# First similarities and maxima of the last stage laid into the end of the middle stage, and its first two silus of the dense layer moved behind ScalarE's first change of table

## The chip, the cores and the metric

The kernel runs on one core of one Trainium2 chip. The metric is the device time of one execution in microseconds (us). A core has five engines that run their own instruction streams and meet at semaphores: TensorE (PE in the rows, with PEld for its weight loads), VectorE (DVE), ScalarE (ACT), GpSimd (POOL) and SyncE (SP), which here only issues transfers. Each engine takes its instructions strictly in the order of its stream.

## The reference

Four residual blocks over 32 sequences of 128 tokens with 128 features. The first two are a cross-attention over a context of 77 and a layer of 16 routed experts. The change lies where the third block ends and the fourth begins:

```python
x = x + _L1_xattn_ref(_layernorm(x), ctx_1024, ctx_1024)        # the middle stage
x = x + _L1_ffn_ref(_layernorm(x), W_up, W_down, W_q, keys, down_embed, up_embed)   # the last stage

# _L1_xattn_ref
scores = jnp.einsum('bqd,bkd->bqk', query, key) * d ** (-0.5)
...
attn = jax.nn.softmax(scores, axis=-1)
return jnp.einsum('bqk,bkd->bqd', attn, value)

# _L1_ffn_ref: 4 heads, two sets of 64 keys, 8 best of each, 8 best of the 64 sums
q = jnp.einsum('btd,ed->bte', hidden_states, W_q)
...
sim = jnp.einsum('pbthn,hkpn->pbthk', q, keys)
scores_xy, idx_xy = jax.lax.top_k(sim, K)
...
scores, pk = jax.lax.top_k(all_scores, K)
indices = jnp.take_along_axis(all_idx, pk, axis=-1)
de = down_embed[indices]
ue = up_embed[indices]
w = jax.nn.silu(jnp.einsum('btd,bthkd->bthk', hidden_states, de) * jax.nn.softmax(scores, axis=-1))
experts_states = jnp.einsum('bthk,bthkd->btd', w, ue)
dense = jnp.einsum('bti,di->btd', jax.nn.silu(jnp.einsum('btd,id->bti', hidden_states, W_up)), W_down)
return dense + experts_states
```

## The kernel before

All orders are written out by hand, one stream for each engine; every buffer is kept twice and `p` (0 or 1) names the copy.

**The middle stage** walks over 8 groups `g` of 4 sequences. TensorE transposes the tokens (`tokens_t`), makes the scores against the context (`scores(g)`), transposes the exponentials (`probabilities_t`) and applies them (`attention`). ScalarE makes the exponentials (`exps(g)`), takes the transposes out of PSUM and computes the reciprocal roots of the next normalisation (`roots3(g)`). VectorE adds the result to the tokens (`add_attention`) and takes their statistics (`statistics3`). GpSimd normalises the tokens of groups 0 to 6 (`last_tokens(g)`, L501); VectorE does that of group 7 (`last_tokens(7)`, L1543). TensorE transposes them (`last_tokens_t(g)`, L1119) and ScalarE writes them to `x3_t` (`last_tokens_out(g)`), which raises `xt3_ready`.

**The last stage** handles 32 tiles of 128 tokens, two in a turn, in 16 turns. For tile `(i, p)`, in the order in which the data flows:

- SyncE copies the tile's columns from `x3_t` into `xt[p]` (`load_d`); for turn `i` it waits until `score_mm` says that the scores of turn `i - 1` have been made from the old `xt[p]`.
- TensorE: `keys` (L1146, all similarities in one matmul), `scores` (L1161) and `last_scores` (L1167), `up` (L1154, the dense layer's first matmuls), `down` (L1179), `back` (L1189, transposes of the weights), `add_experts` (L1198).
- ScalarE: `similarities` (L762 and L552, a part of `keys`' result to SBUF), `exps(i, p)` (L783), `silus` (L791, four heads), `hidden` (L769, the silu of `up`'s result into `h1[p]`). Exponential and silu need different tables, so each turn holds two ACT_TABLE_LOADs (L807, L813).
- VectorE: `near_tops` (L1573 to L1581, the eight best of each head), `best_pairs` (L1598 to L1606), `own_sums` (L1588), `pick` (L1616), `norms`, `tail` (L1629), `result` (L1635).
- GpSimd: `sums` (L512) and `weigh` (L520).

Three dependences matter here. `up(i + 1, p)` writes the bank from which `hidden(i, p)` reads, so it waits for `h1_ready`. `hidden(i + 1, p)` overwrites `h1[p]`, so it waits for `down_mm`, that is, for `down(i, p)`. And ScalarE's turn runs `similarities(i + 1, 1)`, then `exps(i, 1)`, then the change to silu:

```python
            if more:
                similarities(i + 1, 1)
            exps(i, 1)
            act.preload_act_table(ACT.Silu)
            silus(i, 0)
            if more:
                hidden(i + 1, 0)
                hidden(i + 1, 1)
                silus(i, 1)
```

Ahead of turn 0 stand the first `similarities`, the first two `hidden` and a first `exps(0, 0)`; as the roots of the middle stage use the table with logarithm and exponential, the two `hidden` are framed by two loads of their own (L769, L824).

Of the kernel before, what the change touches and what calls it, by code (L numbers as in the profile page):

```python
# [87 lines left out]
def program(nc, a):  # L88
    with ExitStack() as ctx:
# [448 lines left out]
        def _(act):  # L538
# [199 lines left out]

            tokens_out(0)
            roots2(0)  # L740
            tokens_out(1)
            roots2(1)
            for g in range(NB):
                exps(g)
                if g >= 3:
                    last_tokens_out(g - 3)
                if g + 2 < NB:
                    tokens_out(g + 2)
                if g + 2 < NB:
                    roots2(g + 2)  # L750
                probabilities_out(g)
                if g:
                    roots3(g - 1)
            last_tokens_out(NB - 3)
            last_tokens_out(NB - 2)
# [85 lines left out]
        def _(pe):  # L841
# [279 lines left out]

            tokens_t(0)
            tokens_t(1)
            scores(0)
            scores(1)
            tokens_t(2)
            for g in range(NB):
                probabilities_t(g)
                if g + 2 < NB:
                    scores(g + 2)  # L1130
                attention(g)
                if g >= 2:
                    last_tokens_t(g - 2)
                if g + 3 < NB:
                    tokens_t(g + 3)
            last_tokens_t(NB - 2)


            pe.wait_ge(wts_d, 64)

# [115 lines left out]
        def _(dve):  # L1256
# [291 lines left out]
            statistics2(0)
            statistics2(1)
            maximum(0)  # L1550
            biases(0)
            maximum(1)
            biases(1)
            statistics2(2)
            for g in range(NB):
                if g:
                    add_attention(g - 1)
                    statistics3(g - 1)
                shares(g)
                if g + 3 < NB:  # L1560
                    statistics2(g + 3)
                if g + 2 < NB:
                    maximum(g + 2)
                    biases(g + 2)
            add_attention(NB - 1)
            statistics3(NB - 1)
            last_tokens(NB - 1)
# [133 lines left out]
```

## Time and profile before

| | |
|---|---|
| time, median of 3 runs | 469.45 us (469.17 to 470.87) |
| time of the profiled execution | 469.85 us |
| its span from first to last instruction | 468.1 us |
| busy: PE, DVE, ACT, POOL | 401.9, 359.4, 332.9, 336.2 us |
| mean granted TensorE clock | 0.96 of full speed |

The span is what the trace shows; 1.75 us of the profiled execution's time lie outside it. The middle stage ends and the last stage begins between 200 and 240 us. Busy shares over the whole span say little about that stretch; it is read from the instructions in order of time.

### The profile page before, as it was taken

The numbers are of one execution on the slowest core, as the hardware profiler recorded it, in microseconds if no ns is written. First come the engines' busy times: TensorE is split into PE (matmuls) and PEld (weight loads), VectorE is DVE, ScalarE is ACT, GpSimd is POOL, SyncE is SP. The second block draws the span as 40 slices with busy tenths as digits, with TensorE's granted clock in tenths as the row PEclk, the third lists the DMA queues.
The fourth block names the chain that finished last, engine by engine and source line by source line (L and its number), as shares of the span: only waits on it lengthen the run. The fifth ranks groups of instructions, "written<-read, shape, count | busy, mean of one in ns | idle before, by whom it ended". The sixth has DMA issues, their size and how long they took to land.

```text
span 468.1 us, 9533 instructions
## 1 busy us (share of the span) xinstructions
PE 401.9 (86%) x2617; PEld 322.8 (69%) x2617; DVE 359.4 (77%) x1473; ACT 332.9 (71%) x606; POOL 336.2 (72%) x266
## 2 busy tenths in 40 slices
PE   4899898599999787867889988998899988999876
PEld 3687786278998656754666777777767777767766
DVE  3799887323233269976999999999999999999981
ACT  2466353244445057656699999999999999999994
POOL 5226666614655605571899999999999999999993
PEclk9999999599999999869799999999999999999998
DMA  6998022126876160000000000000000000000000
GB/s 186 336 274 242 30 75 92 47 50 201 218 201 190 45 181 7 6 1 12 1 13 23 22 11 15 19 22 22 11 11 22 22 17 16 12 22 22 13 11 13
DMA packets 46515, 32.02 MB, mean 68 GB/s; under 512 B 4155, under 2 KB 42651, under 8 KB 46491
## 3 DMA queue, kind: packets, MB, share of 16 engines
q1 hardware_dynamic: 42635, 25.01, 18.8%
q0 software_dynamic: 2624, 6.43, 3.9%
q10 hardware_dynamic: 1232, 0.31, 0.3%
q8 instruction: 10, 0.16, 0.2%
q14 instruction: 14, 0.11, 0.1%
HBM read 19.02 MB, written 10.62 MB: 63 GB/s over the span
## 4 chain that ended last, share of the span: by engine, by line
POOL 33%; issue 10%; DVE 7%; PE 4%; ACT 3%; POOLq 1%; ACTq 0%; DVEq 0%
POOL arena_sb L520 21%; POOL arena_sb L512 11%; DVE picked_sb L1616 4%; ACT arena_sb L791 1%; PE banks L1146 1%; PE banks L1189 1%; PE banks L1154 1%; POOL xh_sb L501 1%; PE banks L1179 0%; ACT arena_sb L783 0%; PE banks L1198 0%; PE banks L1248 0%; DVE arena_sb L1588 0%; ACT sc_sb L724 0%; POOLq L524 0%
## 5 line engine op out<-in xcount | busy, mean ns | idle before, releaser
L520 POOL TENSOR_TENSOR arena_sb<-arena_sb,picked_sb 128x1096 f32<-128x1096 f32 (+1 forms) x46 | 151.8, 3331 | 10.1 <-DVE picked_sb L1616 10.1
L1616 DVE SCALAR_TENSOR_TENSOR picked_sb<-arena_sb,best_sb,banks 128x548 f32<-128x548 f32 x128 | 90.3, 777 | 0.2 <-POOL arena_sb L512 0.2
L791 ACT ACTIVATE arena_sb<-arena_sb,bsum_sb 128x548 f32<-128x548 f32 x124 | 83.0, 743 | 8.3 <-DVE bsum_sb L1624 7.3
L512 POOL TENSOR_TENSOR arena_sb<-near_sb,sim_y_sb 128x1024 f32<-128x1024 f32 (+1 forms) x32 | 74.1, 2340 | 10.2 <-DVE near_sb L1581 10.2
L1189 PEld LDWEIGHTS banks<-ident_sb,arena_sb 128*128 128x128 f32 x496 | 57.9, 153 | 24.5 <-issue 16.2
L1189 PE MATMUL banks<-ident_sb,arena_sb 128*128 128x128 f32 x496 | 61.9, 279 | 4.8 <-DVE arena_sb L1629 4.8
L783 ACT ACTIVATE arena_sb<-arena_sb 128x2192 f32<-128x2192 f32 x32 | 65.6, 2049 | 0.2
L490 POOL DMA_INDIRECT token_rows<-arena_sb,token_of_sb x32 | 30.7, 960 | 33.4 <-issue 24.7
L1154 PEld LDWEIGHTS banks<-xt_sb,w_up_t_sb 128*128 128x128 f32 x256 | 32.8, 200 | 19.5 <-ACT w_t_sb L552 17.6
L1179 PE MATMUL banks<-w_down_t_sb,h_sb 128*128 128x128 f32 x256 | 36.0, 286 | 8.9 <-DVE x_all_sb L1635 8.9
L1154 PE MATMUL banks<-xt_sb,w_up_t_sb 128*128 128x128 f32 x256 | 36.9, 290 | 6.7 <-ACT w_t_sb L552 6.0
L449 POOL DMA_INDIRECT slot_rows<-x_all_sb,scatter_row_sb x32 | 31.4, 983 | 13.7 <-issue 9.5
L1198 PE MATMUL banks<-up_e_sb,w_t_sb 128*128 128x128 f32 x256 | 35.3, 281 | 5.5 <-DVE picked_sb L1616 4.5
L501 POOL TENSOR_SCALAR xh_sb<-x_all_sb,cmv_sb,crstd_sb 128x128 f32<-128x128 f32 x28 | 21.9, 792 | 25.1 <-ACT crstd_sb L714 25.1
L1458 DVE TENSOR_SCALAR arena_sb<-banks 128x512 f32<-128x512 f32 x16 | 11.1, 691 | 36.7 <-PE banks L1036 36.7
L1179 PEld LDWEIGHTS banks<-w_down_t_sb,h_sb 128*128 128x128 f32 x256 | 31.5, 194 | 11.1 <-issue 11.1
L1146 PE MATMUL banks<-z_sb,xt_sb 128*128 128x512 f32 x64 | 34.7, 628 | 3.1 <-DVE arena_sb L1588 2.3
L1198 PEld LDWEIGHTS banks<-up_e_sb,w_t_sb 128*128 128x128 f32 x256 | 31.0, 191 | 8.5 <-DVE picked_sb L1616 5.2
L1161 PE MATMUL banks<-down_t_sb,xt_sb 128*128 128x512 f32 x64 | 31.3, 612 | 0.0
L1036 PE MATMUL banks<-arena_sb,w_sb 128*128 128x256 f32 x128 | 29.9, 382 | 1.0 <-ACT arena_sb L552 1.0
L1046 PE MATMUL banks<-w_sb,arena_sb 128*128 128x128 f32 x256 | 30.5, 275 | 0.0
L1588 DVE TENSOR_TENSOR arena_sb<-near_sb,banks 128x1024 f32<-128x1024 f32 (+1 forms) x32 | 30.1, 939 | 0.0
(188 smaller groups left out, 826.5 us busy)
## 6 DMA issues: line engine op xcount, KB each, us to landing
w_sb<-w SPq DMA_DIRECT2D x32, 256.0 KB, 3.4
slot_rows<-arena_sb POOLq DMA_DIRECT2D x4, 528.0 KB, 6.4
arena_sb<-slot_rows SPq DMA_DIRECT2D x16, 132.0 KB, 2.3
x_all_sb<-x SPq DMA_DIRECT2D x8, 256.0 KB, 3.7
token_rows<-x_all_sb SPq DMA_DIRECT2D x8, 256.0 KB, 2.8
x_all_sb<-token_rows SPq DMA_DIRECT2D x8, 256.0 KB, 5.1
xt_sb<-x_t_sb SPq DMA_DIRECT2D x32, 64.0 KB, 1.8
out<-x_all_sb SPq DMA_DIRECT2D x32, 64.0 KB, 1.5
```

Source lines behind the costliest of these rows:

```text
L449: pool.indirect_dma_start(out=slots, out_offset=bass.IndirectOffsetOnAxis(ap=scatter_row[i % 2][:, t:t + 1], axis=0), in_=x_all[:, i * TT ...
L512: pool.tensor_tensor(vv[p][:, 0:n, 0:DENSE].rearrange("p h (i j) -> p h i j", i=XI), near[p][:, 0:n, TOP:2 * TOP].unsqueeze(3).broadcast_t ...
L520: pool.tensor_tensor(pp[p][:, heads, :], pp[p][:, heads, :], picked[p][:, heads, :], ALU.mult).then_inc(weighed, 1)
L783: act.activation(pp[p][:, :, :], vv[p][:, :, 0:WIDE], ACT.Exp).then_inc(pp_ready, 1)
L791: ins = act.activation(pp[p][:, h, :], pp[p][:, h, :], ACT.Silu, scale=bsum[p][:, h:h + 1])
L1146: pe.matmul(bank[4 * p + 1][:, :], xt[p][:, :], z1[:, :], start=True, stop=True).then_inc(sim_mm, 1)
L1154: ins = pe.matmul(bank[4 * p][:, c * P:(c + 1) * P], w_up_t[:, c * P:(c + 1) * P], xt[p][:, :], start=True, stop=True)
L1161: ins = pe.matmul(bank[4 * p + 2][:, :], xt[p][:, :], down_t[:, :], start=True, stop=True)
L1179: ins = pe.matmul(results(p), h1[p][:, c, :], w_down_t[:, c, :], start=c == 0, stop=False)
L1189: ins = pe.matmul(bank[4 * p][0:n, c * P:(c + 1) * P], pp[p][:, h, c * P:c * P + n], ident[:, :], is_transpose=True, start=h == 0, stop=h ...
L1198: ins = pe.matmul(results(p), w_t[p][:, c, :], up_e[:, c, :], start=False, stop=c == FC - 1)
L1616: ins = dve.scalar_tensor_tensor(out=picked[p][:, h, :], in0=vv[p][:, h, 0:WIDE], scalar=best[p][:, h, TOP - 1:TOP], in1=scores_of(p), op0 ...
```

## The change

It moves instructions and adds no arithmetic. VectorE, ScalarE and TensorE get a new order between the last groups of the middle stage and the second turn of the last one; the loops of the later turns stay as they are. The functions keep their bodies, apart from the names `context_scores` for the middle stage's `scores` and `exps_of_tables` for the last stage's `exps`. GpSimd's and SyncE's streams are untouched. The core of the diff (definitions that only moved are left out):

```diff
 # ScalarE
             def turn(i, j, more, most=True):
...
                 act.preload_act_table(ACT.Silu)
+                if i is FIRST:
+                    hidden(FIRST, 0)
+                    hidden(FIRST, 1)
                 silus(i, 0)
...
+            similarities(FIRST, 0)
             last_tokens_out(NB - 3)
+            similarities(FIRST, 1)
             last_tokens_out(NB - 2)
...
-            similarities(FIRST, 0)
-            similarities(FIRST, 1)
             roots3(NB - 1)
             last_tokens_out(NB - 1)
-            hidden(FIRST, 0)
-            hidden(FIRST, 1)
-            act.preload_act_table(ACT.Exp)
-            exps(FIRST, 0)
+            exps_of_tables(FIRST, 0)
             similarities(1, 0)
             turn(0, None, True)
 # TensorE
+            for g in range(NB):
+                probabilities_t(g)
+                if g + 2 < NB:
+                    context_scores(g + 2)
+                attention(g)
+                if g >= 2:
+                    last_tokens_t(g - 2)
+                if g + 3 < NB:
+                    tokens_t(g + 3)
+                if g >= NB - 2:
+                    pe.wait_ge(cexp_ready, g + 1)
+                    keys(FIRST, g - (NB - 2))
+            last_tokens_t(NB - 2)
+            pe.wait_ge(wts_d, 64)
             for p in two:
                 scores(FIRST, p)
             last_tokens_t(NB - 1)
+            pe.wait_ge(xt3_ready, NB - 1)
+            up(FIRST, 0)
+            last_scores(0, first=True)
+            keys(1, 0)
             pe.wait_ge(xt3_ready, NB)
-            for p in two:
-                up(FIRST, p)
-                last_scores(p, first=True)
-            keys(1, 0)
+            up(FIRST, 1)
+            last_scores(1, first=True)
             keys(1, 1)
             turn(FIRST, None, True)
 # VectorE
+            near_tops(FIRST, 0)
             add_attention(NB - 1)
             statistics3(NB - 1)
+            best_pairs(FIRST, 0)
+            own_sums(FIRST, 0)
             last_tokens(NB - 1)
...
-            step.turn()
-            for p in two:
-                near_tops(FIRST, p)
-                best_pairs(FIRST, p)
-                own_sums(FIRST, p)
+            near_tops(FIRST, 1)
+            best_pairs(FIRST, 1)
+            own_sums(FIRST, 1)
             pick(FIRST, 0)
             pick(FIRST, 1)
```

**ScalarE, from `last_tokens_out(7)` into turn 0.** Line numbers are those of either file; `h_sb` is `hidden`, the first `arena_sb` row with 128x2192 is the exponential of tile (0, 0), `first_sb` and `sim_y_sb` are `similarities`, `bsum_sb` marks `silus`. Before:

```order
L552 ACTIVATE x_t_sb<-banks 128x512
L769 ACT_TABLE_LOAD
L769 ACTIVATE h_sb<-banks 128x512 x2
L824 ACT_TABLE_LOAD
L783 ACTIVATE arena_sb<-arena_sb 128x2192
L762 ACTIVATE first_sb<-banks 128x4x8
L552 ACTIVATE sim_y_sb<-banks 128x128
L775 ACTIVATE bexp_sb<-best_sb 128x32 x2
L762 ACTIVATE first_sb<-banks 128x4x8
L552 ACTIVATE sim_y_sb<-banks 128x192
L783 ACTIVATE arena_sb<-arena_sb 128x2192
L807 ACT_TABLE_LOAD
```

and from the same place in the changed kernel:

```order
L552 ACTIVATE x_t_sb<-banks 128x512
L764 ACTIVATE arena_sb<-arena_sb 128x2192
L743 ACTIVATE first_sb<-banks 128x4x8
L552 ACTIVATE sim_y_sb<-banks 128x128
L756 ACTIVATE bexp_sb<-best_sb 128x32 x2
L743 ACTIVATE first_sb<-banks 128x4x8
L552 ACTIVATE sim_y_sb<-banks 128x192
L764 ACTIVATE arena_sb<-arena_sb 128x2192
L788 ACT_TABLE_LOAD
L750 ACTIVATE h_sb<-banks 128x512 x2
L772 ACTIVATE arena_sb<-arena_sb,bsum_sb 128x548 x4
```

Two table loads are gone, and the first two `hidden` now stand behind `exps(0, 1)` and the load of turn 0, ahead of `silus(0, 0)`.

**TensorE, from the first `up` to the first `down`.** `w_up_t_sb` is `up`, 128x36 is `last_scores`, `z_sb` is `keys`, `w_down_t_sb` is `down`. Before:

```order
L1154 MATMUL banks<-xt_sb,w_up_t_sb 128x128 x4
L1167 MATMUL banks<-down_t_sb,xt_sb 128x36
L1154 MATMUL banks<-xt_sb,w_up_t_sb 128x128 x4
L1167 MATMUL banks<-down_t_sb,xt_sb 128x36
L1146 MATMUL banks<-z_sb,xt_sb 128x512 x2
L1154 MATMUL banks<-xt_sb,w_up_t_sb 128x128 x8
L1179 MATMUL banks<-w_down_t_sb,h_sb 128x128 x4
```

and in the changed kernel:

```order
L1134 MATMUL banks<-xt_sb,w_up_t_sb 128x128 x4
L1147 MATMUL banks<-down_t_sb,xt_sb 128x36
L1126 MATMUL banks<-z_sb,xt_sb 128x512
L1134 MATMUL banks<-xt_sb,w_up_t_sb 128x128 x4
L1147 MATMUL banks<-down_t_sb,xt_sb 128x36
L1126 MATMUL banks<-z_sb,xt_sb 128x512
L1134 MATMUL banks<-xt_sb,w_up_t_sb 128x128 x8
L1159 MATMUL banks<-w_down_t_sb,h_sb 128x128 x4
```

`keys(1, 0)` now stands between the two halves of `up` and `last_scores`, so `last_scores` of tile (0, 1), whose end lets SyncE load `xt[1]` for `keys(1, 1)`, is queued behind a matmul that itself waits for a load.

**VectorE, from `add_attention(7)` on.** `csum_sb` marks `add_attention`, the next two rows are `statistics3`, `xh_sb` is `last_tokens(7)`, `first_sb` begins `near_tops`. Before:

```order
L1533 SCALAR_TENSOR_TENSOR x_all_sb<-banks,csum_sb,x_all_sb 128x128 x4
L1487 BN_STATS cbn_sb<-x_all_sb 128x6 x4
L1490 BN_AGGR cmv_sb<-cbn_sb 128x2 x4
L1543 TENSOR_SCALAR xh_sb<-x_all_sb,cmv_sb,crstd_sb 128x128 x4
L73 ISA
L1573 MAX first_sb<-banks 128x8 x4
L1576 MAX banks<-banks 128x8 x4
```

and in the changed kernel, where `near_tops(0, 0)` has already ended in the row ahead:

```order
L1531 SCALAR_TENSOR_TENSOR x_all_sb<-banks,csum_sb,x_all_sb 128x128 x4
L1485 BN_STATS cbn_sb<-x_all_sb 128x6 x4
L1488 BN_AGGR cmv_sb<-cbn_sb 128x2 x4
L1573 TENSOR_TENSOR arena_sb<-near_sb,banks 128x4x2x8
L1576 TENSOR_TENSOR arena_sb<-near_sb,banks 128x4x28 x2
L1581 MAX best_sb<-arena_sb 128x8 x4
L1563 TENSOR_TENSOR arena_sb<-near_sb,banks 128x2x512
L1541 TENSOR_SCALAR xh_sb<-x_all_sb,cmv_sb,crstd_sb 128x128 x4
L1548 MAX first_sb<-banks 128x8 x4
```

The work of tile (0, 0) has moved ahead of `last_tokens(7)`, in two pieces around `add_attention(7)` and `statistics3(7)`.

## Rows read from the trace of the kernel before

**Rows 1.** The page's chain that ended last, share of the span by engine.
```profile
POOL 33%; issue 10%; DVE 7%; PE 4%; ACT 3%; POOLq 1%; ACTq 0%; DVEq 0%
```

**Rows 2.** Timeline of VectorE, later turns: start, length (us), line, tiles, [idle before <-releaser].
```profile
237.76 0.31 DVE L1629 TENSOR_REDUCE arena_sb<-arena_sb 128x1 f32<-128x148 f32 x1
238.26 5.65 DVE L1616 SCALAR_TENSOR_TENSOR picked_sb<-arena_sb,best_sb,banks 128x548 f32<-128x548 f32 x8 [0.18 <-POOL arena_sb L512]
...
253.21 5.65 DVE L1616 SCALAR_TENSOR_TENSOR picked_sb<-arena_sb,best_sb,banks 128x548 f32<-128x548 f32 x8
```

**Rows 3.** Timeline of GpSimd.
```profile
206.82 3.12 POOL L501 TENSOR_SCALAR xh_sb<-x_all_sb,cmv_sb,crstd_sb 128x128 f32<-128x128 f32 x4 [0.52 <-ACT crstd_sb L714]
...
256.16 9.80 POOL L520 TENSOR_TENSOR arena_sb<-arena_sb,picked_sb 128x2192 f32<-128x2192 f32 x3 [0.54 <-DVE picked_sb L1616]
```

**Rows 4.** Timeline of VectorE between the stages.
```profile
208.41 1.12 DVE L1533 SCALAR_TENSOR_TENSOR x_all_sb<-banks,csum_sb,x_all_sb 128x128 f32<-128x128 f32 x4 [1.69 <-PE banks L1107]
...
214.65 1.11 DVE L1543 TENSOR_SCALAR xh_sb<-x_all_sb,cmv_sb,crstd_sb 128x128 f32<-128x128 f32 x4 [3.70 <-ACT crstd_sb L714]
215.68 0.58 DVE L1573 MAX8 first_sb<-banks 128x8 f32<-128x56 f32 x4
...
217.75 0.22 DVE L1598 TENSOR_TENSOR arena_sb<-near_sb,banks 128x64 f32<-128x64 f32 x1
...
218.78 1.20 DVE L1588 TENSOR_TENSOR arena_sb<-near_sb,banks 128x1024 f32<-128x1024 f32 x1
219.90 0.58 DVE L1573 MAX8 first_sb<-banks 128x8 f32<-128x56 f32 x4
...
223.57 5.65 DVE L1616 SCALAR_TENSOR_TENSOR picked_sb<-arena_sb,best_sb,banks 128x548 f32<-128x548 f32 x8
```

**Rows 5.** Timeline of ScalarE between the stages.
```profile
217.13 1.28 ACT L769 ACT_TABLE_LOAD   x1
218.43 0.60 ACT L769 ACTIVATE h_sb<-banks 128x512 f32<-128x512 f32 x1
...
220.10 1.28 ACT L824 ACT_TABLE_LOAD   x1
...
225.88 0.20 ACT L762 ACTIVATE first_sb<-banks 128x32 f32<-128x32 f32 x1 [1.97 <-PE banks L1146]
...
226.19 2.03 ACT L783 ACTIVATE arena_sb<-arena_sb 128x2192 f32<-128x2192 f32 x1
...
231.52 2.68 ACT L791 ACTIVATE arena_sb<-arena_sb,bsum_sb 128x548 f32<-128x548 f32 x4 [2.00 <-DVE bsum_sb L1624]
...
235.06 2.68 ACT L791 ACTIVATE arena_sb<-arena_sb,bsum_sb 128x548 f32<-128x548 f32 x4
```

**Rows 6.** Timeline of TensorE between the stages; each matmul counts as two instructions.
```profile
204.41 1.13 PE L1098 MATMUL banks<-ident_sb,sc_sb 128*77 128x128 f32 x4
...
209.99 1.11 PE L1119 MATMUL banks<-ident_sb,xh_sb 128*128 128x128 f32 x4 [0.83 <-POOL xh_sb L501]
...
217.17 1.16 PE L1154 MATMUL banks<-xt_sb,w_up_t_sb 128*128 128x128 f32 x8 [0.69 <-ACT x_t_sb L552]
218.16 0.31 PE L1167 MATMUL banks<-down_t_sb,xt_sb 128*128 128x36 f32 x2
...
220.39 1.13 PE L1146 MATMUL banks<-z_sb,xt_sb 128*128 128x512 f32 x2 [0.80 <-DMA xt_sb<-x_t_sb]
223.80 2.05 PE L1146 MATMUL banks<-z_sb,xt_sb 128*128 128x512 f32 x2 [2.28 <-DVE arena_sb L1588]
225.64 3.62 PE L1154 MATMUL banks<-xt_sb,w_up_t_sb 128*128 128x128 f32 x16
```

**Rows 7.** Windows: stretch, length, busy us and count of PE, PEld, DVE, ACT, POOL, clock.
```profile
212.00:213.00 1.00, 1.00 (x2) 0.39 (x2) 0.00 (x0) 0.16 (x2) 0.00 (x0) 0.58 0.00 0
...
222.00:224.00 2.00, 0.20 (x1) 0.23 (x2) 1.97 (x9) 1.91 (x5) 2.00 (x1) 0.77 0.00 0
...
228.00:230.00 2.00, 2.00 (x11) 2.00 (x11) 1.97 (x8) 1.50 (x2) 2.00 (x1) 0.53 0.00 0
```

More of the change, by code:

```diff
@@ L737, in last_tokens_out @@
                      bank[4 * (g % 2)][:, :].rearrange("p (b t) -> p b t", b=BT))
[L739 to L755, printed above, removed]
             def similarities(i, p):
@@ L775, in best_exps, with exps_of_tables @@
                     act.activation(bexp[p][:, :, :], best[p][:, :, :], ACT.Exp).then_inc(bexp_ready, 1)
-            def exps(i, p):
+            def exps_of_tables(i, p):
                 act.wait_ge(best_ready, 1 + 2 * i + p + 1)
@@ L805, in turn @@
                     similarities(i + 1, 1)
-                exps(i, 1)
+                exps_of_tables(i, 1)
                 act.preload_act_table(ACT.Silu)
+                if i is FIRST:
+                    hidden(FIRST, 0)
+                    hidden(FIRST, 1)
                 silus(i, 0)
@@ L813, in turn @@
                     act.preload_act_table(ACT.Exp)
-                    exps(i + 1, 0)
+                    exps_of_tables(i + 1, 0)
                     if most:
                         similarities(i + 2, 0)
+            tokens_out(0)
+            roots2(0)
+            tokens_out(1)
+            roots2(1)
+            for g in range(NB):
+                exps(g)
+                if g >= 3:
+                    last_tokens_out(g - 3)
+                if g + 2 < NB:
+                    tokens_out(g + 2)
+                if g + 2 < NB:
+                    roots2(g + 2)
+                probabilities_out(g)
+                if g:
+                    roots3(g - 1)
             similarities(FIRST, 0)
+            last_tokens_out(NB - 3)
             similarities(FIRST, 1)
+            last_tokens_out(NB - 2)
             roots3(NB - 1)
             last_tokens_out(NB - 1)
-            hidden(FIRST, 0)
-            hidden(FIRST, 1)
-            act.preload_act_table(ACT.Exp)
-            exps(FIRST, 0)
+            exps_of_tables(FIRST, 0)
             similarities(1, 0)
@@ L1079, in tokens_t, with context_scores @@
                 ins.then_inc(cxnt_mm, 1)
-            def scores(g):
+            def context_scores(g):
                 p = g % 2
@@ L1120, in last_tokens_t @@
                 ins.then_inc(xt3_mm, 1)
[L1122 to L1139, printed above, removed]
             def keys(i, p):
@@ L1222, in turn @@
                         keys(i + 2, 1)
-            pe.wait_ge(cexp_ready, NB)
-            keys(FIRST, 0)
-            keys(FIRST, 1)
+            tokens_t(0)
+            tokens_t(1)
+            context_scores(0)
+            context_scores(1)
+            tokens_t(2)
+            for g in range(NB):
+                probabilities_t(g)
+                if g + 2 < NB:
+                    context_scores(g + 2)
[9 more added lines that the diff above has]
+            pe.wait_ge(wts_d, 64)
             for p in two:
@@ L1545, in last_tokens @@
                 ins.then_inc(cxh_ready, 1)
-            step.turn()
[L1548 to L1567, printed above, removed]
             def near_tops(i, p):
@@ L1659, in _ @@
             step.turn()
-            for p in two:
-                near_tops(FIRST, p)
-                best_pairs(FIRST, p)
-                own_sums(FIRST, p)
+            statistics2(0)
+            statistics2(1)
+            maximum(0)
+            biases(0)
+            maximum(1)
+            biases(1)
+            statistics2(2)
+            for g in range(NB):
+                if g:
+                    add_attention(g - 1)
+                    statistics3(g - 1)
+                shares(g)
+                if g + 3 < NB:
+                    statistics2(g + 3)
+                if g + 2 < NB:
+                    maximum(g + 2)
+                    biases(g + 2)
+            near_tops(FIRST, 0)
+            add_attention(NB - 1)
+            statistics3(NB - 1)
+            best_pairs(FIRST, 0)
+            own_sums(FIRST, 0)
+            last_tokens(NB - 1)
+            near_tops(FIRST, 1)
+            best_pairs(FIRST, 1)
+            own_sums(FIRST, 1)
             pick(FIRST, 0)
```

## The prediction, made from these rows

> **What bounds the kernel now.** I began with the chain that ended last: GpSimd has the largest share of it [rows 1]. That is only the last link seen from the end, so I looked at one whole turn. `pick`, the last piece of VectorE's turn, starts at 238.26 and again at 253.21 us [rows 2]: a turn lasts 14.95 us. GpSimd's `weigh` waits 0.54 us in it for `pick` [rows 3], while VectorE, at its worst place in the first turn, waits 0.18 us [rows 2]. So VectorE sets the pace, by a small margin. The change leaves the loops alone; every later turn starts 14.95 us after the one before, and the end moves by as much as `pick(1, 0)` at 238.26 moves. The question is when that instruction can start.
>
> Then I read the timelines of the four engines between 204 and 240 us. VectorE stands idle 3.70 us ahead of `last_tokens(7)` and 1.69 us ahead of `add_attention(7)` [rows 4]: there is room for the work that the change moves. ScalarE makes two table loads of 1.28 us, but later waits 1.97 us for `keys(1, 1)` and 2.00 us for the norms [rows 5]. TensorE waits for a transfer ahead of `keys(1, 0)` and for VectorE's `own_sums(0, 1)` ahead of `keys(1, 1)` [rows 6]. Last come the clocks: TensorE is at half its speed (1.2 GHz) until about 212.84, at 2.4 GHz until about 223.08, and low again until about 229.88; the three times follow from means of 0.58, 0.77 and 0.53 in windows that hold one step each [rows 7].
>
> **The change, part by part.**
>
> *VectorE's tile (0, 0) moved up.* `keys(0, 0)` goes ahead of `probabilities_t(7)`, which starts at 204.41. At the lower clock `keys` takes the stream 1.84 us (223.80 to 225.64), at the higher one about half [rows 6]. I take 1.7. What stands behind it is late by that: `roots3(6)`, and GpSimd's `last_tokens(6)` goes from 206.82 to about 208.5 [rows 3]. `similarities(0, 0)` take 0.3 (225.88 to 226.19 [rows 5]), so `near_tops(0, 0)` starts near 208.9. Its 2.07 us (215.68 to 217.75 [rows 4]) end at 211.0. `add_attention(7)` then starts at 211.0 in place of 208.41; with the statistics it takes 2.54 (208.41 to 210.95, where the wait of 3.70 begins), to 213.5. `best_pairs` and `own_sums` of tile (0, 0), 2.15 (217.75 to 219.90), end at 215.7, `last_tokens(7)`, 1.03, at 216.7, and tile (0, 1), 3.67 (219.90 to 223.57), at 220.4. `pick(0, 0)` would start 3.2 us early (223.57 before). `last_tokens(7)` itself ends 1.0 late. `keys(0, 1)` pushes back `last_tokens_t(6)` too, but the roots behind it are due at 216, so that is covered; without this cover it would cost up to a `keys`, 1.84. The `sums` of GpSimd and SyncE's stream keep their order and cost nothing: GpSimd idles until `near_tops` is done in either kernel.
>
> *TensorE's `keys(1, 0)` between the two `up`.* After `last_tokens(7)` come four transposes, about 0.6 (1.11 at the lower clock [rows 6]), to 217.3. `up(0, 0)` no longer waits 0.69 for `last_tokens_out(7)`; its 0.99 (217.17 to 218.16) end at 218.3. From there to `keys(1, 0)` 2.23 us pass (218.16 to 220.39: `last_scores`, SyncE's issue and the transfer), to 220.5. `keys` takes about 1.0, `up(0, 1)` 0.99, to 222.5, and now the same 2.23 come a second time, because `last_scores(1)`, which frees `xt[1]`, was queued behind `keys(1, 0)`: `keys(1, 1)` starts at 224.7. It was 223.80. The lead of 3.2 us on VectorE is lost on this chain of two transfers. `keys(1, 1)` ends at 225.8 at the higher clock (1.13) or 226.7 at the lower (2.05); before, 225.85.
>
> *ScalarE.* Two loads go, 2 x 1.28 = 2.56 us of its own time [rows 5]. But `exps(0, 1)` stands behind `similarities(1, 1)`, which wait for `keys(1, 1)`. So it starts at 226.15 or 227.1 (226.19 before), and the saved loads turn into a longer wait there. `exps(0, 1)` and the load end 3.35 later (2.03 and 1.28), then come both `hidden`, 0.60 each and overlapping a little, 1.05 together. `silus(0, 0)` starts at 230.55 or 231.45 (231.52 before) and ends 2.68 later, at 233.2 or 234.1.
>
> The Trainium skill, page "ScalarE: Activation LUTs", section "What ACT_TABLE_LOAD costs", counts a drain of about 1.38 us on top of a load of 1.28, and its rules ask for batching by table. By that the change would save 5.3 us of ScalarE's time. The rows have no such drain: the load at 217.13 ends at 218.41 and the silu starts at 218.43 [rows 5]. By either price it is time in which ScalarE would wait for `keys(1, 1)`.
>
> *The dense layer behind it.* This is the part that I expect to decide. `up(1, 0)` waits for `hidden(0, 0)`, which now ends at 230.1 or 231.0. Before, `up(1, 0)` and `up(1, 1)` ran from 225.64 for 3.62 us [rows 6] and `down` behind them, well ahead of `hidden(1, 0)`. Now `up(1, 0)`, `up(1, 1)` and `down(0, 0)` must pass between `hidden(0, 0)` and `hidden(1, 0)`, and `down(0, 1)` ahead of `hidden(1, 1)`. Each is a group of four matmuls, 0.99 at the higher clock and 1.81 (3.62 / 2) at the lower. TensorE has nothing to do from the end of `keys(1, 1)` until then, over 4 us; before, 1.13 us of matmul between waits of 0.80 and 2.28 were enough for the clock to fall [rows 6, 7]. So these groups start low. How long they stay low is bounded by the two returns in the trace: 2.8 us after gapless work began (209.99 to 212.84) and 6.1 us (223.80 to 229.88) [rows 6, 7].
>
> With `hidden(0, 0)` at 230.1 and the clock back after 2.8 us: 1.55 groups at 1.81, then 1.45 at 0.99, 0.15 for the result to land: `down(0, 0)` is done at 234.5, `last_scores` and `down(0, 1)` 1.15 later, `hidden(1, 1)` 0.55 after that. `silus(0, 1)` starts at 236.2 against 235.06: +1.1. With the clock back after 6.1 us it is 237.55: +2.5. If `keys(1, 1)` was low, both are 0.9 more: +2.0 and +3.4.
>
> From there nothing changes: `silus(0, 1)`, 2.68, then `tail(0, 1)` at 237.76 and `pick(1, 0)` at 238.26 [rows 2], all later by the same amount. `weigh(0, 1)`, for which the second half of these silus waits, starts behind `exps(0, 1)` by 228.2 to 229.2 and takes half of 9.80 [rows 3], to 233.1 to 234.1: no wait.
>
> **Sum.** -3.2 on VectorE, used up by the second transfer; -2.56 on ScalarE, used up by the same wait; +1.1 to +3.4 from `up` and `down` on the path. The middle of the four values is 2.25; I take +2.1, since 1.7 for `keys(0, 0)` is near its upper end. On the profiled execution's 469.85 that makes 471.95. That execution is 0.4 above the median of the runs shown, 469.45; on the median it is **471.5**.
>
> **Rivals.**
>
> *The lower clock comes earlier.* From 213 on TensorE's work is thinner than before: a wait for `last_tokens(7)`, then two transfers. If it falls to 1.2 GHz already there, `up(0, 0)`, `keys(1, 0)` and `up(0, 1)` cost 0.8 to 0.9 more each. For it: the fall at 223.08. Against: `up` and `keys` still fill a good part of that stretch. Two of the three add 1.7, in all +3.8: 473.3. The Trainium skill, page "TensorE: Matmul & The Clock Gate", section "Loop structure matters more than you think", warns of just this, matmuls with a transfer to wait for between them; the trace of before has one such place, and the clock fell behind it.
>
> *The clock is back at once, or doesn't fall.* Then three groups take 3.1 and fit beside `silus(0, 0)`, and `silus(0, 1)` moves by -0.1 to +0.8: about 469.8. Against it: over 4 us without a matmul.
>
> *Faster: the saved loads count.* If `keys(1, 1)` came early enough that ScalarE need not wait for it, `exps(0, 1)` would start up to 2.6 earlier and the whole turn with it: 466.9. It decides from the point where the second transfer takes under about half of its 2.23, and the groups behind `hidden(0, 0)` run at the higher clock. By the skill's drain it would be up to 5.3, 464.2. Against both: the one such transfer in the trace took 2.23.
>
> *Nothing moves.* The later turns could take back a part: GpSimd's wait of 0.54 is such a slack, VectorE's stream shows none. About 469.5.
>
> **How the numbers follow.** The forecast (+1.1 to +3.4) gets 0.60, the lower clock earlier 0.16, the clock back at once 0.14, faster 0.06, nothing 0.04. The bound of 0.5%, about what a measurement of this kernel can tell from no change, is 2.35 us: 467.1 and 471.8. Of the forecast, 0.24 lie above 471.8 and 0.36 below. Slower: 0.24 + 0.16 = 0.40. Same: 0.36 + 0.14 + 0.04 = 0.54. Faster: 0.06. The range leaves out the faster case and the upper half of the earlier clock: 469.0 to 473.5; the forecast's own is 470.5 to 472.9.
>
> **What would show it.** Right: `pick(0, 0)` near 220, `keys(1, 1)` waiting for a transfer of `xt` and starting at 224 or later, ScalarE idle some 3 to 5 us ahead of `similarities(1, 1)`, ScalarE's silus of `hidden(1, *)` waiting for L1159, the clock low around 230, `pick(1, 0)` at 239.4 to 241.7, and turns of 14.95 after it. Wrong: `keys(1, 1)` before 223, a clock of 1.00 at 230 to 234, no wait ahead of `hidden(1, 0)`, or turns of another length, which would mean that the pace is set by what I have not looked at.

## The result, and the profile after

The changed kernel takes 473.05 us in the median of 17 runs (468.70 to 475.06), the kernel before 469.73 beside it (467.71 to 471.85, 17 runs). The ratio of times is 1.0045, with a 95% interval of 1.0023 to 1.0066: about 2.1 us slower. The two medians stand 3.3 us apart; as the runs of either kernel scatter over 4 to 6 us, I go by the ratio and its interval. The forecast was 2.1 us slower, 471.5 in a range of 469.0 to 473.5.

The profiled execution took 474.34 us, 4.5 more than the one of before (469.85), which is twice the ratio. The first thing to settle is therefore how much of it lies in the stretch that was changed. The edit begins behind `probabilities_t(6)`, so I look there first, on TensorE's timeline of the kernel before:

```profile
97.32 3.69 PE L1036 MATMUL banks<-arena_sb,w_sb 128*128 128x256 f32 x16
...
200.62 0.66 PE L1098 MATMUL banks<-ident_sb,sc_sb 128*77 128x128 f32 x4 [1.35 <-ACT sc_sb L724]
```

TensorE's timeline after; the lines of the program have moved up by two here:

```profile
97.46 5.38 PE L1034 MATMUL banks<-arena_sb,w_sb 128*128 128x256 f32 x16
...
202.64 0.66 PE L1096 MATMUL banks<-ident_sb,sc_sb 128*77 128x128 f32 x4 [1.57 <-ACT sc_sb L724]
...
218.61 0.66 PE L1117 MATMUL banks<-ident_sb,xh_sb 128*128 128x128 f32 x4 [1.94 <-DVE xh_sb L1541]
219.10 1.06 PE L1134 MATMUL banks<-xt_sb,w_up_t_sb 128*128 128x128 f32 x8
...
222.21 1.13 PE L1126 MATMUL banks<-z_sb,xt_sb 128*128 128x512 f32 x2 [1.91 <-DMA xt_sb<-x_t_sb]
223.17 1.05 PE L1134 MATMUL banks<-xt_sb,w_up_t_sb 128*128 128x128 f32 x8
...
226.31 1.12 PE L1126 MATMUL banks<-z_sb,xt_sb 128*128 128x512 f32 x2 [1.93 <-DMA xt_sb<-x_t_sb]
231.77 3.78 PE L1134 MATMUL banks<-xt_sb,w_up_t_sb 128*128 128x128 f32 x16 [4.34 <-ACT h_sb L750]
235.34 1.91 PE L1159 MATMUL banks<-w_down_t_sb,h_sb 128*128 128x128 f32 x8
```

`probabilities_t(6)` is 2.02 us late before the edit has had any effect. Most of it arises at 97 us, in the expert layer of the second block: the same 16 instructions take 5.38 us in place of 3.69. TensorE's clock was at half there, as the last section shows. So I count every time of after from `probabilities_t(6)`: 2.02 is taken off before it is compared. From there to `pick(1, 0)` this profile has 39.66 us against 37.64 (238.26 [rows 2] less 200.62): **+2.02**.

The rows above show how. `keys(1, 0)` waits 1.91 us for a transfer, `keys(1, 1)` 1.93 us for the next one, and then TensorE waits 4.34 us for ScalarE's `h_sb`, that is for `hidden(0, 0)`; before, `up` followed `keys(1, 1)` without a gap [rows 6]. What became of the two waits on ScalarE's own timeline after:

```profile
223.37 0.20 ACT L743 ACTIVATE first_sb<-banks 128x32 f32<-128x32 f32 x1 [1.56 <-PE banks L1126]
...
227.47 0.20 ACT L743 ACTIVATE first_sb<-banks 128x32 f32<-128x32 f32 x1 [3.50 <-PE banks L1126]
...
227.78 2.03 ACT L764 ACTIVATE arena_sb<-arena_sb 128x2192 f32<-128x2192 f32 x1
229.82 1.28 ACT L788 ACT_TABLE_LOAD   x1
231.12 1.08 ACT L750 ACTIVATE h_sb<-banks 128x512 f32<-128x512 f32 x2
232.09 2.67 ACT L772 ACTIVATE arena_sb<-arena_sb,bsum_sb 128x548 f32<-128x548 f32 x4
237.35 0.60 ACT L750 ACTIVATE h_sb<-banks 128x512 f32<-128x512 f32 x1 [2.59 <-PE banks L1159]
238.88 0.60 ACT L750 ACTIVATE h_sb<-banks 128x512 f32<-128x512 f32 x1 [0.93 <-PE banks L1159]
239.37 2.67 ACT L772 ACTIVATE arena_sb<-arena_sb,bsum_sb 128x548 f32<-128x548 f32 x4
```

The two table loads of before are gone. ScalarE waits 3.50 us for `keys(1, 1)`, where it waited 1.97 [rows 5], and `exps(0, 1)` is 0.43 us earlier than before (227.78 - 2.02 = 225.76 against 226.19). Then come the new waits, 2.59 and 0.93 us for L1159, `down`. `silus(0, 1)`, the last row, starts 36.73 us after `probabilities_t(6)`; before it was 235.06 - 200.62 = 34.44: +2.29.

VectorE's timeline after:

```profile
210.91 0.59 DVE L1548 MAX8 first_sb<-banks 128x8 f32<-128x56 f32 x4 [1.63 <-ACT sim_y_sb L552]
...
222.15 5.65 DVE L1591 SCALAR_TENSOR_TENSOR picked_sb<-arena_sb,best_sb,banks 128x548 f32<-128x548 f32 x8
...
242.07 0.31 DVE L1604 TENSOR_REDUCE arena_sb<-arena_sb 128x1 f32<-128x148 f32 x1 [4.24 <-ACT arena_sb L772]
242.30 5.64 DVE L1591 SCALAR_TENSOR_TENSOR picked_sb<-arena_sb,best_sb,banks 128x548 f32<-128x548 f32 x8
...
257.65 5.65 DVE L1591 SCALAR_TENSOR_TENSOR picked_sb<-arena_sb,best_sb,banks 128x548 f32<-128x548 f32 x8 [0.32 <-issue]
```

`pick(0, 0)` is 3.44 us earlier (222.15 - 2.02 = 220.13 against 223.57 [rows 4]), and nothing comes of it: the `tail` waits 4.24 us for ScalarE's silus, and `pick(1, 0)` stands behind it. From there to the next `pick` it is 15.35 us, not 14.95; the turns behind it have 14.96, against 14.95 before.

TensorE's clock after, in windows (stretch, length, busy us and count of PE, PEld, DVE, ACT and POOL, clock):

```profile
226.00:228.00 2.00, 1.12 (x2) 0.30 (x2) 2.00 (x6) 0.53 (x3) 2.00 (x1) 0.94 0.00 0
...
230.00:232.00 2.00, 0.23 (x1) 0.23 (x2) 1.90 (x16) 1.99 (x3) 2.00 (x1) 0.50 0.00 0
...
236.00:238.00 2.00, 2.00 (x11) 2.00 (x11) 1.80 (x9) 0.60 (x1) 2.00 (x2) 0.50 0.00 0
238.00:240.00 2.00, 2.00 (x12) 1.42 (x12) 0.00 (x0) 1.12 (x2) 1.53 (x1) 1.00 0.00 0
```

It falls to 1.2 GHz at about 227.8, just behind `keys(1, 1)`, and is back at 238.0, 6.2 us after `up(1, 0)` began. All of `up(1, p)` and most of `down(0, p)` ran at half speed.

### The profile page after: what moved, and what is told of

Read it like the earlier page. It is cut to its first block, busy times and chain, and to the rows that moved or that the text cites. A ratio compares the mean times of both kernels' runs of the same rounds, so it can differ in the third digit from the quotient of the medians.

```text
span 472.6 us, 9530 instructions
## 1 busy us (share of the span) xinstructions
PE 401.9 (85%) x2617; PEld 323.4 (68%) x2617; DVE 359.4 (76%) x1473; ACT 330.2 (70%) x604; POOL 336.3 (71%) x266
## 4 chain that ended last, share of the span: by engine, by line
POOL 32%; issue 10%; DVE 5%; PE 4%; ACT 2%; DMA 1%; POOLq 1%; ACTq 0%
POOL arena_sb L520 21%; POOL arena_sb L512 11%; DVE picked_sb L1591 4%; PE banks L1134 1%; ACT arena_sb L772 1%; ACT arena_sb L764 1%; DMA xt_sb<-x_t_sb 1%; PE banks L1169 1%; PE banks L1159 1%; PE banks L1126 0%; PE banks L1246 0%; PE banks L1178 0%; POOLq L524 0%; PE banks L1141 0%; DVE arena_sb L1563 0%
## 5 line engine op out<-in xcount | busy, mean ns | idle before, releaser
L1159 PE MATMUL banks<-w_down_t_sb,h_sb 128*128 128x128 f32 x256 | 36.8, 290 | 8.9 <-DVE x_all_sb L1610 8.9
L1159 PEld LDWEIGHTS banks<-w_down_t_sb,h_sb 128*128 128x128 f32 x256 | 32.2, 198 | 11.2 <-issue 11.2
L1034 PE MATMUL banks<-arena_sb,w_sb 128*128 128x256 f32 x128 | 31.6, 397 | 1.0 <-ACT arena_sb L552 1.0
```

The costliest lines, as they stand in the source:

```text
L1034: ins = pe.matmul(bank[2 + 2 * (b % 2) + c // 2][:, (c % 2) * CAP:(c % 2 + 1) * CAP], w1[b][:, c * P:(c + 1) * P], xe_t[b % 2][:, :], star ...
L1159: ins = pe.matmul(results(p), h1[p][:, c, :], w_down_t[:, c, :], start=c == 0, stop=False)
```

## The experiments

What I compare is the stretch from `probabilities_t(6)` to `pick(1, 0)` in the profile of each, 37.64 us before and 39.66 after, and the ratio of times to the kernel before, run beside each, with its interval. One profile of each was taken. Two profiles of the changed kernel differ by 1.6 us in the stretch, by TensorE's clock alone, so a stretch is read together with its rows and its ratio, and a difference of a few tenths carries nothing.

**The order on TensorE put back.** The changed kernel, with both `up` ahead of both `keys` again:

```diff
  up(FIRST, 0); last_scores(0, first=True)
- keys(1, 0)
  pe.wait_ge(xt3_ready, NB)
  up(FIRST, 1); last_scores(1, first=True)
+ keys(1, 0)
  keys(1, 1)
```

> The changed kernel with TensorE's old order: both up(0, p) and last_scores(p) first, then keys(1, 0) and keys(1, 1), so that the two transfers of xt overlap. Measured from the start of probabilities_t(6) to that of pick(1, 0): 37.64 us in the kernel before, 39.66 in the changed one. My theory (second transfer, then up and down at the lower clock behind hidden(0, p)): keys(1, 1) waits no 1.9 us for its transfer and starts some 2.5 us earlier, exps(0, 1) with it, the clock is still low behind hidden(0, 0); the stretch is 37.1 (36.6 to 37.7), the time 2.0 to 3.0 us below the changed kernel and about that of before. Rival (the loss comes from keys and near_tops laid ahead of the middle stage's last groups, or from hidden alone): the stretch stays at 39.2 to 40.1.

The stretch was 36.47 us, 0.1 under the lower end of what was expected, the ratio 0.9970 (0.9939 to 1.0002). TensorE's timeline of it:

```profile
220.28 2.23 PE L1126 MATMUL banks<-z_sb,xt_sb 128*128 128x512 f32 x4 [0.80 <-DMA xt_sb<-x_t_sb]
226.84 3.78 PE L1134 MATMUL banks<-xt_sb,w_up_t_sb 128*128 128x128 f32 x16 [4.33 <-ACT h_sb L750]
```

There is one wait for a transfer, 0.80 us, and both `keys` follow it together: the second transfer runs beside the first. `exps(0, 1)` starts 22.15 us after `probabilities_t(6)` (222.84 less 200.69), against 25.14 in the changed kernel: that is what the second transfer costs, 2.99 us, and 3.19 by the end of the stretch. The wait of 4.33 us for `hidden(0, 0)` is still there, and `up` behind it still takes 3.78 us at the lower clock.

**TensorE kept busy behind `keys(1, 1)`, in the changed order.** Four matmuls whose result nobody reads:

```diff
  keys(1, 1)
+ pe.wait_ge(picked_ready, 1 + 1)
+ for _ in range(4):
+     pe.matmul(bank[2][:, :], centre[:, :], ctx_row[:, 0:512], start=True, stop=True)
```

> The changed kernel with four matmuls of 128x512 that nothing reads, behind keys(1, 1), into a bank that is free by then, to keep TensorE busy until hidden(0, 0). Added work: about 3.7 us of TensorE, in time in which it waits. My theory: the clock is 1.00 when up(1, 0) starts, the four groups take about 1.0 each and not 1.8, ScalarE's waits of 2.59 and 0.93 ahead of hidden(1, p) shrink to 0.3 and 0.7; the stretch to pick(1, 0) is 37.2 (36.8 to 37.8) against 39.66, the time 2 to 3 us below the changed kernel. Rival (the place of hidden costs by its order alone, the clock is a bystander): 39.2 to 39.7. Second rival (the extra matmuls do not keep the clock, or reach past hidden(0, 0)): 39.5 to 40.5.

The stretch was 39.57 us, a miss of 2.4 us, and inside the ranges of both rivals; the ratio was 1.0004 (0.9973 to 1.0035). TensorE's timeline of it shows why the stretch tells less than it was meant to:

```profile
218.58 1.87 PE L1134 MATMUL banks<-xt_sb,w_up_t_sb 128*128 128x128 f32 x8
...
222.65 2.08 PE L1126 MATMUL banks<-z_sb,xt_sb 128*128 128x512 f32 x2 [1.92 <-DMA xt_sb<-x_t_sb]
224.51 1.92 PE L1134 MATMUL banks<-xt_sb,w_up_t_sb 128*128 128x128 f32 x8
...
228.63 2.07 PE L1126 MATMUL banks<-z_sb,xt_sb 128*128 128x512 f32 x2 [1.93 <-DMA xt_sb<-x_t_sb]
230.50 4.49 PE L1236 MATMUL banks<-ctx_t_sb,centre_sb 128*128 128x512 f32 x8
235.04 2.05 PE L1134 MATMUL banks<-xt_sb,w_up_t_sb 128*128 128x128 f32 x16
```

In this execution the clock was low from `up(0, 0)` on (1.87 for 1.06 us), through both `keys`: the case that the prediction had as the rival of a lower clock that comes earlier. `keys(1, 1)` was late by that, and the gain went there. Behind the added matmuls `up(1, 0)` and `up(1, 1)` took 2.05 us in place of 3.78, and from the start of `hidden(0, 0)` to `silus(0, 1)` it is 5.30 us (234.39 to 239.69) against 8.25 (231.12 to 239.37). So behind the added matmuls the clock was back, against both rivals: the part behaved as the theory had it, and the stretch as a whole doesn't separate it from the rest. By the ratios the kernel is about 1.9 us below the changed one (1.0004 against 1.0045), near the 2 to 3 us expected, but the two intervals overlap. So it was done again in the other order, below.

**ScalarE's part alone.** The kernel before, with only the two `hidden` moved behind the load of silu's table, and the two loads gone:

```diff
  # in ScalarE's turn, behind preload_act_table(Silu)
+ if i is FIRST:
+     hidden(FIRST, 0); hidden(FIRST, 1)
  ...
- hidden(FIRST, 0); hidden(FIRST, 1)
- act.preload_act_table(ACT.Exp)
  exps(FIRST, 0)
```

> The kernel before with only ScalarE's part on the tables: the first two hidden behind the load of turn 0, the two loads of their own gone; VectorE and TensorE as before. My theory: exps(0, 1) stays at its place because it waits for keys(1, 1), up(1, 0) starts some 4 to 5 us later than before and finds the lower clock; the stretch is 39.1 to 40.1 against 37.64, the time 1.5 to 2.5 us above before. Rival (two loads off ScalarE's stream count): 35.1 to 37.4, the time up to 2.6 us below before.

The stretch was 40.27 us, 0.2 over the upper end of what was expected, the ratio 1.0037 (1.0007 to 1.0067). Two fewer loads and a slower kernel: on TensorE's timeline of it `up` has the same wait and the same low clock.

```profile
226.51 1.60 PE L1146 MATMUL banks<-z_sb,xt_sb 128*128 128x512 f32 x2 [2.29 <-DVE arena_sb L1588]
232.45 3.79 PE L1154 MATMUL banks<-xt_sb,w_up_t_sb 128*128 128x128 f32 x16 [4.33 <-ACT h_sb L769]
```

Only half of the 2.63 us above before is the edit's. VectorE's timeline has `pick(0, 0)`, which doesn't depend on `hidden`:

```profile
226.29 5.65 DVE L1616 SCALAR_TENSOR_TENSOR picked_sb<-arena_sb,best_sb,banks 128x548 f32<-128x548 f32 x8
```

That is 24.28 us after `probabilities_t(6)` (202.01 here), against 22.95 before: 1.33 us arise ahead of the edit. In the middle stage the clock came back at about 216.7 here, 14.7 us after `probabilities_t(6)`, and at 212.84 before, 12.2 us after it:

```profile
216.00:218.00 2.00, 2.00 (x5) 0.71 (x3) 0.64 (x3) 0.81 (x4) 0.00 (x0) 0.82 0.00 0
```

From `pick(0, 0)` to `pick(1, 0)` it is 15.99 us against 14.69: +1.30, which is the edit's, and in line with the ratio.

**VectorE's part alone.** The old order on TensorE, and both `hidden` at their old place with both loads; what is left of the change is tile (0, 0) laid early, with the `keys` and `similarities` that lead to it:

```diff
  # to the kernel with the order put back
- if i is FIRST:
-     hidden(FIRST, 0); hidden(FIRST, 1)
  ...
+ hidden(FIRST, 0); hidden(FIRST, 1)
+ act.preload_act_table(ACT.Exp)
  exps_of_tables(FIRST, 0)
```

> The changed kernel with the first two hidden at their old place (two loads of their own again) and TensorE's old order of up and keys: what stays of the change is the work of the first tiles laid into the middle stage. My theory: VectorE's lead of 3 us or more comes through; up(1, 0) follows keys(1, 1) without a pause, no wait ahead of hidden(1, p); the stretch is 34.1 (33.6 to 35.0) against 37.64 before, the time 3 to 4 us below before. Rival (the moved keys and near_tops cost as much in the middle stage as they save): 37.0 to 38.0. Second rival (the two loads are on the path once VectorE is early): 35.5 to 36.8.

The stretch was 34.91 us, the ratio 0.9916 (0.9885 to 0.9948). This is the part of the change that pays. TensorE's timeline has no wait ahead of `up(1, 0)` any more, and the full clock:

```profile
222.28 1.95 PE L1134 MATMUL banks<-xt_sb,w_up_t_sb 128*128 128x128 f32 x16
```

On GpSimd's timeline of it, what waits next:

```profile
223.58 9.78 POOL L520 TENSOR_TENSOR arena_sb<-arena_sb,picked_sb 128x2192 f32<-128x2192 f32 x3 [2.47 <-ACT arena_sb L764]
```

`weigh(0, 0)` now waits for `exps(0, 0)`, which stands behind the two loads and both `hidden`.

**The new order on TensorE, `hidden` at its old place.** The same edit to the changed kernel itself:

> The changed kernel with the first two hidden at their old place (two loads of their own again), but TensorE's new order kept, keys(1, 0) between the two up. With the kernels changed (stretch from probabilities_t(6) to pick(1, 0): 39.66), pair_order (36.47) and hidden_back (34.91) it fills the table of the two moves. My theory: the second transfer holds keys(1, 1) and through it exps(0, 1); hidden(0, 1) waits for the late up(0, 1), so the load behind it and exps(0, 0) come later, weigh(0, 0) with them; no wait for L1159 ahead of hidden(1, p). The stretch is 36.6 (36.0 to 37.4). Rival (the order matters only together with the moved hidden, because the lower clock is what costs): 34.9 to 35.5.

The stretch was 37.50 us, 0.1 over the upper end, the ratio 0.9976 (0.9951 to 1.0002). With 34.91 above it prices the order, but by another way than in the changed kernel. On ScalarE's timeline of it:

```profile
224.40 0.60 ACT L750 ACTIVATE h_sb<-banks 128x512 f32<-128x512 f32 x1 [2.46 <-PE banks L1134]
```

`hidden(0, 1)` waits for `up(0, 1)`, which stands behind `keys(1, 0)` and its transfer, and holds up the second load, `exps(0, 0)` and GpSimd's `weigh(0, 0)`, 2.6 us in all. So the first transfer in the new order costs about as much here as the second one did with `hidden` moved.

**`exps(0, 0)` first, then both `hidden`.** The kernel with VectorE's part alone, but with the two loads and both `hidden` behind `exps(0, 0)`, where GpSimd doesn't wait for them:

```diff
- hidden(FIRST, 0); hidden(FIRST, 1)
- act.preload_act_table(ACT.Exp)
  exps_of_tables(FIRST, 0)
+ hidden(FIRST, 0); hidden(FIRST, 1)
+ act.preload_act_table(ACT.Exp)
```

> hidden_back with exps(0, 0) ahead of the first two hidden and of their two loads (it can use the table of the middle stage): GpSimd can start weigh(0, 0) when pick(0, 0) is done and need not wait for exps(0, 0). My theory: weigh(0, 0) 0.5 to 0.8 us earlier, VectorE without its waits of 0.55 and 0.19 us ahead of pick(1, 0): stretch 34.2 (34.0 to 34.6), the time 3.4 to 4 us below before. Rival (the loads behind exps(0, 0) push similarities(1, 1) and exps(0, 1) back): 35.0 to 36.0.

The stretch was 34.22 us, the ratio 0.9899 (0.9853 to 0.9945). On GpSimd's timeline the wait for ScalarE is gone:

```profile
223.36 9.80 POOL L520 TENSOR_TENSOR arena_sb<-arena_sb,picked_sb 128x2192 f32<-128x2192 f32 x3 [1.75 <-DVE picked_sb L1591]
```

**TensorE kept busy, in the old order.** The kernel with TensorE's order put back (36.47 us), `hidden` where the change puts it, and the four matmuls with their wait behind `keys(1, 1)`:

> The changed kernel with TensorE's old order of up and keys and four matmuls of 128x512 that nothing reads behind keys(1, 1) (3.7 us of added work of TensorE at the higher clock, in time in which it waits). My theory: the clock is 1.00 behind hidden(0, 0), the waits of 1.58 and 0.73 us ahead of hidden(1, p) in pair_order go, the stretch is 34.3 (34.0 to 35.0) against 36.47. Rival (the place of hidden costs by its order alone): 36.0 to 36.7.

The stretch was 34.24 us, the ratio 0.9885 (0.9848 to 0.9922), the six runs within 0.8 us (465.27 to 466.06). TensorE's timeline of it:

```profile
223.62 3.70 PE L1236 MATMUL banks<-ctx_t_sb,centre_sb 128*128 128x512 f32 x8 [0.64 <-DVE picked_sb L1594]
227.32 2.05 PE L1134 MATMUL banks<-xt_sb,w_up_t_sb 128*128 128x128 f32 x16
```

And on ScalarE's, the silus behind it, which no longer wait for `down`:

```profile
231.23 1.05 ACT L750 ACTIVATE h_sb<-banks 128x512 f32<-128x512 f32 x2
```

Up to `exps(0, 1)` the two kernels agree to 0.01 us, and no other edit divides them: 3.70 us of work that nobody needs, laid where TensorE had none, take 2.23 us off the stretch, and the two intervals of the ratio (0.9939 to 1.0002 without it) don't overlap. With it the place of `hidden` costs nothing.

**The changed kernel once more.**

> The changed kernel once more, beside the others on the same chip: the stretch is 39.7 if the clock falls between keys(1, 1) and hidden(0, 0), as in its first profile (38.7 to 40.7, by how soon the clock returns), up to 42 if it falls ahead of keys(1, 0). The time is 1 to 4 us above before.

The stretch was 38.04 us, 0.7 under the lower end; the ratio 1.0055 (1.0026 to 1.0083), with a median of 473.38. All waits stand where they stood in the first profile, but two are shorter, on ScalarE's timeline:

```profile
236.22 0.60 ACT L750 ACTIVATE h_sb<-banks 128x512 f32<-128x512 f32 x1 [1.39 <-PE banks L1159]
237.34 0.60 ACT L750 ACTIVATE h_sb<-banks 128x512 f32<-128x512 f32 x1 [0.52 <-PE banks L1159]
```

Its windows say why: the clock came back at about 234.7, 2.8 us after `up(1, 0)` began at 231.84, not 6.2.

```profile
232.00:234.00 2.00, 2.00 (x10) 2.00 (x11) 1.37 (x9) 2.00 (x4) 2.00 (x2) 0.50 0.00 0
234.00:236.00 2.00, 2.00 (x18) 2.00 (x17) 1.14 (x2) 0.83 (x2) 2.00 (x2) 0.83 0.00 0
```

All of them together. Two parts of the stretch are given: from `probabilities_t(6)` to `exps(0, 1)`, and from there to `silus(0, 1)`. VectorE's work is laid early in all but the first and the fifth row; of the fifth, 1.33 us belong to the middle stage's clock.

| kernel | TensorE's order | `hidden` | to `exps(0, 1)` | on to `silus(0, 1)` | stretch, us | ratio to before (95%) |
|---|---|---|---|---|---|---|
| before | old | old place | 25.57 | 8.87 | 37.64 | 1 |
| changed | new | moved | 25.14 | 11.59 | 39.66 | 1.0045 (1.0023 to 1.0066) |
| changed, again | new | moved | 25.13 | 9.98 | 38.04 | 1.0055 (1.0026 to 1.0083) |
| order put back | old | moved | 22.15 | 11.40 | 36.47 | 0.9970 (0.9939 to 1.0002) |
| ScalarE's part alone | old | moved | 26.45 | 10.90 | 40.27 | 1.0037 (1.0007 to 1.0067) |
| `hidden` put back | new | old place | 26.25 | 7.99 | 37.50 | 0.9976 (0.9951 to 1.0002) |
| VectorE's part alone | old | old place | 23.66 | 7.99 | 34.91 | 0.9916 (0.9885 to 0.9948) |
| `exps(0, 0)` first | old | in between | 23.66 | 7.35 | 34.22 | 0.9899 (0.9853 to 0.9945) |
| busy, new order | new | moved | 28.00 | 8.64 | 39.57 | 1.0004 (0.9973 to 1.0035) |
| busy, old order | old | moved | 22.14 | 8.87 | 34.24 | 0.9885 (0.9848 to 0.9922) |

The kernels with `exps(0, 0)` first and with TensorE busy in the old order are about 1% faster than the kernel before; their medians are 465.61 and 465.58 us.

## Why the prediction was right

**The parts.** The step from before to VectorE's part alone takes 2.73 us off the stretch (37.64 to 34.91): the lead on VectorE is real. As the stretch before can move by the 1.33 us of the middle stage's clock, the ratio is the surer sign: 0.9916, that is 3.9 us, with 2.4 to 5.4 by its interval. The new order puts 2.59 back (34.91 to 37.50), or 2.99 by `exps(0, 1)` with `hidden` moved. Moving `hidden` adds 2.16 in the new order (37.50 to 39.66; 0.54 in the second profile, where the clock came back sooner) and 1.56 in the old one. The table shows what happens there: `exps(0, 1)` gains 1.1 or 1.5 us, since two loads and two silus no longer stand ahead of it (26.25 to 25.14, 23.66 to 22.15), and the way on to `silus(0, 1)` gets 3.4 to 3.6 us longer (7.99 to 11.40 and 11.59), or 0.9 with TensorE kept busy (8.87).

**VectorE.** `near_tops(0, 0)` came at 208.89 by before's times (208.9 predicted), `pick(0, 0)` at 220.13 (220.4), 3.44 us early where 3.2 were worked out.

**The second transfer.** `keys(1, 0)` and `keys(1, 1)` each wait for one, 1.91 and 1.93 us. `keys(1, 1)` started at 224.29 where 224.7 was predicted. It ran at the higher clock, the better of the two cases that were kept open.

**ScalarE.** The two loads are gone and the wait is longer, as predicted; ScalarE's part alone, slower by 0.37%, shows that taking them out is no gain by itself: `keys(1, 1)` starts 0.22 us behind `pick(0, 0)` there, and 0.23 before, and `exps(0, 1)` waits for it in both. That they are free was too simple, though. Where VectorE's lead reaches ScalarE, their going is worth the 1.1 to 1.5 us above. The page "ScalarE: Activation LUTs" of the Trainium skill, section "What ACT_TABLE_LOAD costs", has a drain of about 1.38 us on top of each load. This trace doesn't agree: the load at 229.82 starts 0.01 us after the exponential ahead of it ends, takes 1.28, and the next silu starts 0.02 us after its end.

**The dense layer.** `hidden(0, 0)` held up `up(1, 0)`, the clock was low, and `silus(0, 1)` moved by +2.29. The prediction had two returns of the clock, after 2.8 and 6.1 us, and with `keys(1, 1)` at the higher clock +1.1 and +2.5 from them. The two profiles of the changed kernel have one each: 6.2 us and +2.29, 2.8 us and +0.67 (237.83 less 202.72 for its `probabilities_t(6)`, against 34.44). That most of the price is the clock, and not the groups themselves, is shown by the four matmuls in the old order; in the new order only the part behind `hidden(0, 0)` shows it (5.30 us for 8.25). The prediction kept the clock's return open between two values that it had read from before, and the measured returns lie at or between them to 0.1 us: 2.8 and 6.2 us in the changed kernel, and by their windows about 5.8 with the order put back and 4.8 with ScalarE's part alone.

**Luck in the number.** The mechanism held step by step, but that the ratio's 2.1 us meets the forecast's +2.1 to the tenth is luck. It was the middle of four cases from +1.1 to +3.4; two of them, with `keys(1, 1)` at the lower clock, occurred in neither profile of this kernel, and the earlier fall that was a rival did occur in the kernel with four added matmuls. The median of 473.05 lies 0.45 us below the upper end of the range.

**Where it was off.** "From there nothing changes ... all later by the same amount" failed by 0.4 us. `pick(1, 0)` moved by 2.02 and the next by 2.42 (55.01 against 52.59 from `probabilities_t(6)`). The first turn is not VectorE's: on GpSimd's timeline after, `weigh(1, 0)` waits for `exps(1, 0)`, which follow `silus(0, 1)` and a load.

```profile
245.55 9.81 POOL L520 TENSOR_TENSOR arena_sb<-arena_sb,picked_sb 128x2192 f32<-128x2192 f32 x3 [6.02 <-ACT arena_sb L764]
```

`weigh(1, 0)` is 2.29 us later than before (241.24 there), like ScalarE's chain, and the `sums` behind it, for which the next `pick` waits, 2.27 (255.29 against 251.00). So GpSimd, held up by ScalarE, sets the next `pick`; the last 0.32 us of its wait have no releaser in the profile. `pick(1, 0)` shows less than the 2.29, for the most part since before it also waited 0.18 us for GpSimd [rows 2].

**What stays open.** Of the 4.5 us between the two profiles 2.42 are the change, 2.02 lie ahead of it. Where the change meets a low clock it scatters, +2.42 and +0.79 at the second `pick` in the two profiles, so the 2.1 us of the ratio are a mean over such cases. The 2.02 us ahead of it are open: `probabilities_t(6)` comes at 200.4 to 201.2 us in five of the ten profiles, before among them, and at 202.0 to 203.1 in the other five. Those five are the four with the new order on TensorE (changed, changed again, `hidden` put back, busy) and ScalarE's part alone. The instructions up to there are the same in all. Against a lasting cost speaks the kernel with the new order and `hidden` at its old place: its second `pick` comes 52.58 us after `probabilities_t(6)`, like before's 52.59, and its ratio is 0.9976, where 2 us ahead of the stretch in every run would make 1.004. But ten single profiles don't say that the change has no part in it.

## What to carry to other kernels

Work that is laid earlier on one engine helps only as far as the next producer follows: here the buffer that `keys(1, 1)` needs was freed by an instruction that had been queued behind `keys(1, 0)`, and VectorE's lead, worth 2.7 us in the stretch, went into the wait for that second transfer. When loads, waits or instructions are taken out of an engine, look at what stood beside them: if the engine waits for the same thing afterwards, little is gained, and what it used to feed early (`hidden`, and so TensorE) now starts late. Where a gap on TensorE can't be closed and short dependent groups follow it, idle-time matmuls that nobody reads can be worth more than they cost (2.23 us in the old order; in the new one, where the clock had fallen ahead of them, no gain clear of noise); if the work can be ordered so that there is no gap, that does as well (34.22 against 34.24 us).
